# Transposing the attention probabilities on VectorE in 32 by 32 blocks, and a context product split into 32 by 32 array tiles

## What is computed

```
def layer0(x, y, mask, Wq, bq, Wk, bk, Wv, bv):       # one head, masked, 77 keys
    scores = (x @ Wq.T + bq) @ (y @ Wk.T + bk).T
    scores = where(mask == 0, -1e9, scores)
    return softmax(scores) @ (y @ Wv.T + bv) + x

def layer1(query, y, W_qkv, b_qkv, W_o, b_o, gamma, beta):   # 16 heads of 32 channels
    Q, K, V = heads(query @ Wq.T + bq), heads(y @ Wk.T + bk), heads(y @ Wv.T + bv)
    context = softmax(Q @ K.T / sqrt(32)) @ V
    z = join(context) @ W_o.T + b_o + query
    return (z - mean(z)) / sqrt(var(z) + 1e-5) * gamma + beta

out = layer1(layer0(x, ctx, mask, ...), ctx, ...)
```

## Time and profile before

| | us |
|---|---|
| time before, median of 3 runs | 393.39 (391.55 to 395.25) |
| the profiled execution's own time | 394.95 |
| its span, first to last instruction | 393.0 |
| PE busy in the span | 377.4 |
| DVE busy | 295.1 |
| ACT busy | 245.9 |
| POOL busy | 222.0 |

### The profile page before, as it was taken

How to read it: one execution, slowest core, us unless ns; L and a number is a source line. 1 busy time by engine, 2 the same in 40 slices (tenths; PEclk the granted TensorE clock), 3 DMA queues, 4 the chain that set the end, 5 groups by cost and what they waited for, 6 DMA issues and landing times.

```text
span 393.0 us, 11993 instructions
## 1 busy us (share of the span) xinstructions
PE 377.4 (96%) x4860; PEld 286.7 (73%) x4860; DVE 295.1 (75%) x711; ACT 245.9 (63%) x749; POOL 222.0 (56%) x245
## 2 busy tenths in 40 slices
PE   8999998899999999999999999999999999799894
PEld 7878956577777787777777777778777777577663
DVE  0446587568867997799977996799778997457886
ACT  2343778765588666866487558856686648556820
POOL 0520655435647764785578664785478647733541
PEclk9999999999999999999999999999999999899999
DMA  8937410530042322522152224222243113322022
GB/s 309 392 125 231 123 39 20 189 107 4 18 157 98 98 71 65 176 94 64 44 177 77 85 72 155 99 98 72 83 147 118 30 57 92 138 97 71 19 107 107
DMA packets 22461, 42.52 MB, mean 108 GB/s; under 512 B 3685, under 2 KB 5221, under 8 KB 22279
## 3 DMA queue, kind: packets, MB, share of 16 engines
q1 hardware_dynamic: 21866, 41.06, 31.8%
q10 hardware_dynamic: 540, 0.69, 0.5%
HBM read 26.49 MB, written 8.39 MB: 89 GB/s over the span
## 4 chain that ended last, share of the span: by engine, by line
PE 82%; ACT 9%; DMA 4%; DVE 3%; issue 1%; SPq 0%; DVEq 0%
PE ps_q L1035 21%; PE ps_out L1124 21%; PE ps_t L1063 11%; PE ps_s L1049 7%; PE ps_pv L1099 6%; PE ps_out L995 5%; ACT prob L563 3%; ACT y L600 2%; PE ps_s L961 2%; DMA pt<-pt 2%; ACT pt L574 1%; PE ps_s L1142 1%; PE ps_s L974 1%; DMA raw<-in_w0k 1%; ACT q L524 1%
## 5 line engine op out<-in xcount | busy, mean ns | idle before, releaser
L418 POOL TENSOR_TENSOR prob<-prob,rc 128x308 f32<-128x308 f32 x128 | 91.9, 725 | 113.5 <-DVE rc L785 112.8
L563 ACT ACTIVATE prob<-ps_s,mx 128x77 f32<-128x77 f32 x512 | 120.5, 334 | 3.5 <-DVE mx L776 3.3
L574 ACT ACTIVATE pt<-ps_t 122x512 f32<-122x512 f32 (+2 forms) x93 | 55.6, 598 | 56.1 <-PE ps_t L1063 53.0
L783 DVE TENSOR_REDUCE sm<-prob 128x4 f32<-128x308 f32 x128 | 59.5, 465 | 25.6 <-ACT prob L563 25.1
L776 DVE TENSOR_REDUCE mx<-ps_s 128x4 f32<-128x308 f32 x128 | 53.7, 465 | 17.8 <-PE ps_s L1049 17.8
L1063 PE MATMUL ps_t<-ident,prob 128*122 128x128 f32 (+1 forms) x372 | 58.3, 279 | 1.7 <-ACT pt L574 1.6
L392 POOL TENSOR_TENSOR x_l<-x_raw,x_h 128x512 fp32r<-128x512 f32 x32 | 44.4, 1390 | 21.0 <-ACT x_h L506 10.8
L1063 PEld LDWEIGHTS ps_t<-ident,prob 128*122 128x122 f32 (+1 forms) x372 | 46.1, 153 | 13.0 <-issue 3.7
L1035 PE MATMUL ps_q<-x_h,wq_h 128*128 128x512 f32 x128 | 53.4, 417 | 0.0
L1035 PE MATMUL ps_q<-x_h,wq_l 128*128 128x512 f32 x128 | 53.0, 414 | 0.0
L1049 PEld LDWEIGHTS ps_s<-k1T,q 32*64 32x64 f32 x2048 | 26.2, 133 | 28.0 <-issue 15.9
(11 more groups left out here) (134 smaller groups left out, 616.9 us busy)
## 6 DMA issues: line engine op xcount, KB each, us to landing
x_raw<-in_xT SPq DMA_DIRECT2D x14, 512.0 KB, 4.4
y<-in_x SPq DMA_DIRECT2D x28, 256.0 KB, 3.0
out<-y SPq DMA_DIRECT2D x28, 256.0 KB, 2.3
pt<-pt SPq DMA_DIRECT2D x31, 90.0 KB, 2.6
pt<-pt SPq DMA_DIRECT2D x31, 64.0 KB, 2.0
mask_sb<-in_mask SPq DMA_DIRECT2D x8, 154.0 KB, 4.7
raw<-in_w0q SPq DMA_DIRECT2D x4, 256.0 KB, 5.3
x_raw<-in_xT SPq DMA_DIRECT2D x1, 1024.0 KB, 7.7
```

Source lines behind the costliest of these rows:

```text
L418: nc.gpsimd.tensor_tensor(ap, ap, wide(rc[:, k % 2, h], KEYS), ALU.mult).then_inc(prob_done, 1)
L563: e = nc.scalar.activation(prob[:, k % 2, t, h], ps_s[:, h, t * KEYS:(t + 1) * KEYS], ACT.Exp, bias=mx[:, k % 2, h, t:t + 1])
L574: nc.scalar.activation(pt[0:n, c], ps_t[0:n, :], ACT.Copy).then_inc(pt_ready, 1)
L783: nc.vector.reduce_sum(sm[:, k % 2, h], prob[:, k % 2, :, h], AX_X).then_inc(sum_done, 1)
```

## The change

- `prob` and `pt` get three blocks of 32 columns for each head (77 padded to 96; POOL zeroes the 19 padding columns once). DVE transposes two heads at a time for all four tiles in one instruction (`nc.vector.transpose`, 4 x 6 blocks of 32 by 32, 768 elements on each partition), two instructions in a unit. The PE transposes, ACT's moves of `ps_t` and SP's two DMAs in each unit go.
- A 32 by 32 block stays in its quadrant of partitions: after it, each quadrant of 32 partitions holds the keys of its own 32 rows of x. So `v1` is spread to all four quadrants (seven DMAs, once), and the context of a unit is made of 48 products of 32x32 weights and 128 columns: two halves of 24, each with 3 key parts x 2 quadrants x 4 heads. The two quadrants of a half go to two banks (`ps_ab`). Output and query products stand between the halves.
- The sums of the exponentials come from the exponential itself (`accum_out` on ACT); DVE's reduction goes.
- The rounding of x to `x_h` moves from DVE to ACT (4 instructions in a block).
- The context's rounding and rest are queued one step sooner (`round_ct(i, k - 1)`, `ct_rest(i, k - 1)` at the end of step `k`), and the output of block `b - 1` starts in group 0 with 8 of its 56 products. The residual of the fourth tile moves to the head of DVE's step for group 0.
- In unit 0 the projection of V stands ahead of the next unit's query and ACT moves it after the exponentials. The last unit's order is rewritten along the same lines; tiles 2 and 3 of the block before the last go through ACT and POOL like all others.

```diff
-OUT_END = {0: (0, 2, 5, 8), 1: (8, 14, 19, 24), 2: (24, 28, 35, 42), 3: (42, 46, 51, 56)}
-OUT_AT = {1: (0, 14, 18, 22), 2: (22, 28, 36, 42), 3: (42, 44, 51, 56)}
+OUT_AT = {0: (0, 0, 4, 8), 1: (8, 14, 18, 22, 26), 2: (26, 28, 34, 38, 42), 3: (42, 44, 49, 51, 53, 56)}
...
-        pt = sb("pt", [P, CHUNKS, BLOCK])
-        pt_1 = sb("pt_1", [KEYS, BLOCK])
-        prob = sb("prob", [P, 2, TILES, GROUP_HEADS, KEYS])
+        pt = sb("pt", [P, GROUP_HEADS, PARTS, TILES, Q])
+        prob = sb("prob", [P, 2, TILES, GROUP_HEADS, PADDED])
...
                 for t in range(TILES):
-                    e = nc.scalar.activation(prob[:, k % 2, t, h], ps_s[:, h, t * KEYS:(t + 1) * KEYS], ACT.Exp, bias=mx[:, k % 2, h, t:t + 1])
+                    e = nc.scalar.activation(prob[:, k % 2, t, h, 0:KEYS], ps_s[:, h, t * KEYS:(t + 1) * KEYS], ACT.Exp,
+                                             bias=mx[:, k % 2, h, t:t + 1], accum_out=sm[:, k % 2, h, t:t + 1])
...
+            def transposes(i, k, a):            # on VectorE
...
+                own = slice(2 * a, 2 * a + 2)
+                wait(dve, prob_done, heads(i, k, 2 * a + 1) + 1)
+                wait(dve, pv_done, units(i, k))
+                nc.vector.transpose(pt[:, own].rearrange("p h n t r -> p t (h n) r"),
+                                    prob[:, k % 2, :, own].rearrange("p t h (n r) -> p t (h n) r", r=Q)).then_inc(t_done, 1)
...
+            def context(i, k, half):            # on TensorE
...
+                if half == 0:
+                    wait(pe, t_done, pairs(i, k, PAIRS))
+                    wait(pe, ctl_ready, units(i, k))
...
+                for n in range(PARTS):
+                    depth = Q if n + 1 < PARTS else LEFT
+                    for side in range(2):
+                        r = 2 * half + side
+                        keys = slice(r * Q, r * Q + depth)
+                        to = context_of(ps_ab[:, :, 0:CT])[:, side].rearrange("p (t j) r -> p j t r", j=HALVES)[:, half]
+                        for h in range(GROUP_HEADS):
+                            own = slice(g * P + h * HEAD_DIM, g * P + (h + 1) * HEAD_DIM)
+                            mm = nc.tensor.matmul(to[h * HEAD_DIM:(h + 1) * HEAD_DIM], v1[keys, b % 2, slot(r, n), own], pt[keys, h, n],
+                                                  start=(n == 0), stop=(n == PARTS - 1))
...
# TensorE's step: before each unit had scores, three transposes, query, output, context(k - 1); now
+                elif g == 0:
+                    query(i, k + 1, 0, 7)
+                    layer0(i, b + 1)
+                    query(i, k + 1, 7, 12)
+                    context(i, k - 1, 0)
+                    query(i, k + 1, 12, QUERY)
+                    part(1)
+                    context(i, k - 1, 1)
+                    part(2)
+                elif g < 3:
+                    part(0)
+                    query(i, k + 1, 0, 12)
+                    part(1)
...
+                    context(i, k - 1, 0)
+                    query(i, k + 1, 12, QUERY)
+                    part(2)
+                    context(i, k - 1, 1)
+                    part(3)
...
# VectorE's step, its new beginning
+                if g == 0:
+                    residual(i, b - 2, 3)
+                    statistics(i, b - 2, 3)
                 if g == 3:
                     residual(i, b - 1, 2)
...
+                for h in range(GROUP_HEADS):
+                    largest(i, k, h)
+                inverse_sums(i, k, 0)
+                if g == 1:
+                    residual(i, b - 1, 0)
+                if g == 2:
+                    residual(i, b - 1, 1)
+                if g == 3:
                     p0_rest(i, b + 1)
+                transposes(i, k - 1, 0)
+                inverse_sums(i, k, 1)
+                transposes(i, k - 1, 1)
...
+                ct_rest(i, k - 1)
```

523 lines of the change are left out of this document (222 added, 301 removed).

## The result

The changed kernel takes 406.96 us (median of 4 runs, 404.98 to 407.20) against 393.44 for the kernel before (4 runs in the same session): a ratio of 1.033, 95% interval 1.028 to 1.039. The forecast was 379 us, faster, with a range of 368 to 408; the measured time lies near its far end and on the other side of no change. The profiled execution has a span of 405.2 us, 12.2 more than the 393.0 of before.

What follows compares the result with a forecast made beforehand. PE was taken to bound the steady blocks, 42.6 us falling to 41.1. Blocks -10.1, transfer -3.5, opening +1.5 and tail -2.2 made -14.3: span 378.7 of 393.0, 379 on the median, range 368 to 408.

Steps and rivals of the forecast that it cites:

- What bounds the kernel: In the steady blocks PE has no slack; its work sums to 42.4 us a block, which is the window.
- Terms 1 and 2: In a block, three PE transposes in each unit go, 5.6 us, and the old contexts go, 4.4 us.
- Term 5: The context in 32x32 tiles on PE costs 0.88 us a half, 7.0 in a block; dear end 13.2.
- Rival C: Eight small tiles on PE do not run side by side: context 1.62 us a half, 409 in all; chance 0.13.
- Rival A: ACT's accumulate costs its whole small row, 0.205 us more for each exponential: 403 in all; chance 0.14.
- Terms 6 and 7: A DVE transpose takes 0.90 us start to start; an ACT exponential with accumulated sum 0.31 instead of 0.21.
- moving the sums off DVE: DVE's sums, 7.4 us of DVE in a block, are hidden behind PE, so removing them is worth nothing by itself.
- The waits: PE's contexts wait for DVE's second transpose in a block's first unit, partly in the second: 1.5 us a block.
- Term 4: SP's two transfers in each unit go; near the end one cost a 2.02 us wait and lower clock: 3.5 gone.
- Opening: Units 1 to 3 become 8.7 us by ACT, and unit 0 waits 1 to 2 for V's rounding: together +1.5.
- Tail: From the last scores' end to the last tile's statistics: 24.0 us before, 21.7 after, so -2.2.

Runs made afterwards that it cites:

- b: Changed kernel with 8 instead of 24 products in each context half, the other two key parts left out: 383.27 us, ratio 0.971.
- c: Changed kernel with one head of each pair transposed on DVE, the other left out: 405.02 us, ratio 1.029.
- h: Kernel before with `accum_out` on ACT's exponentials and without DVE's sums: 402.48 us, ratio 1.019.
- a: Changed kernel with the sums of the probabilities back on DVE and no accumulated output on the exponentials: 422.34 us, ratio 1.068.
- q: Kernel before with 128 more instructions in PE's stream and the 1 MB load of the last residual rows two units later: 388.99 us, ratio 0.986.
- g: d plus `wo_ready` waited for at 2 before the first output products and both context halves of unit 28 behind its output products: 401.64 us, ratio 1.016.
- d: Changed kernel with SP storing the last-but-one block's fourth tile behind the last block's four stores: 404.54 us, ratio 1.026.
- l: g with another order in the last step of all engines, SP's stores included: 403.43 us, ratio 1.022.
- j: Changed kernel with 128 more instructions ahead of everything in PE's stream: 403.85 us, ratio 1.0225.
- e: Changed kernel with the two context halves back to back, at the second one's place, in every unit: 411.84 us, ratio 1.041.
- i: e with 128 more instructions ahead of everything in PE's stream: 400.42 us, ratio 1.014.
- k: e with 64 more instructions ahead of everything in PE's stream: 410.38 us, ratio 1.041.

## Why the prediction was wrong, point by point

*What bounds the kernel.* Right: PE's work, before and after (b, c). But the sum that stood for it, 42.4 as the window is, gave the handovers to the wrong owners. Start to start over one clean block, added up by form from the timelines:

```
us in one block        full x112  context  scores  layer 0  transposes  together
before                   27.5       4.2      3.5     2.2       4.8        42.2
changed                  29.3       6.9      3.6     2.3       0.4        42.5
```

112 full products are 26.1 at 0.233. The rest, 1.4 before and 3.2 after, is what they lose beside small tiles and transposes, with the short waits.

*Terms 1 and 2, what goes.* Forecast 5.6 + 4.4 = 10.0, measured 4.4 + 4.2 = 8.6 in the columns of the transposes and the context, and 0.7 in the first column (0.08 behind the second and third transposes of each unit): 9.3. The 0.09 ahead of the old context and the 0.08 behind the first transposes stay when these go, since the scores pay them.

*Term 5, the context.* This is the step that failed first: "so I take the scores' end: 0.88 for a half", entry and exit included, although the prediction had "plus some 0.2 of entry and exit" just ahead of it. A half is 0.86 to 0.87 and 0.2 more on the full products: 1.06, 8.5 a block instead of 7.0. Of that 0.030 is each product, against 0.0275 for the scores, and 0.33 is fixed, twice in a unit. The rule quoted there, that a change of tiling mode drains the engine, speaks of just this, and the rows priced it at 0.2, part of which they also show behind the PE transposes; cutting the context in two and parting it from the scores made three such changes of one. Rival C (409 us) came close to the measured 407 by luck: it had a half at 1.62 and PE at 45.5 in a block, where 1.06 and 42.2 were measured, and nothing at the ends. Its mechanism is not what happened: at 0.030 a product, against the 0.062 that it took from layer 0, the small tiles do run side by side. Rival A's 403 is as little borne out, with exponentials at 0.30.

*Terms 6 and 7, transpose and accumulate.* Right in size (0.96, 0.30). That moving the sums off DVE is worth nothing was wrong in both directions: h and a show that ACT has no room for the sums in the kernel before and DVE none in the changed one.

*The waits.* 1.5 a block was forecast; the first unit of a clean block waits 0.2, and c gained 0.15, because PE was not 3 us shorter. Where it was 3.8 shorter (b), 1.0 came. The unit without layer 0 waits 2.7. So the block's two errors had opposite signs: PE's work 2.6 over the forecast's 39.6, the waits 1.3 under.

*Term 4, the transfer.* 3.5 is right for units 28 to 30 (q), and it went. A wait for DVE in the same unit, 2.7 and 1.6 of clock (g), took its place. The text said that the context waits for DVE in a block's first unit; it did not ask what happens in the one that has no layer 0.

*Opening.* +1.5 on units 1 to 3 and -1.5 on 4 to 7 were forecast, +3.4 came: 1.6, 0.5, 1.2 and 1.0 of waits, where the kernel before has 2.7 in all, and a clock of 0.85 from 60 to 80, against a block gain that does not exist. How much of it is the clock stays open.

*Tail.* -2.2 forecast, +5.0 measured, 2.8 of it SP's order (d); of the rest, two of DVE's four last rows at 1.65 instead of 0.75 are 1.8 (read from the rows; l, which tried to mend it, did not). This is the second step that failed: the forecast counted PE's queue and ended at the statistics; POOL's and SP's queues behind it were not followed, although the change moved two tiles' last rows from DVE to POOL.

*Not in the sum at all.* PE's stalls without a releaser, by the evidence above for instructions: 3.1 us in the changed kernel's scores and layer 0 against 0.8 before; 0.8 and 0.3 lie in its fourth block and 1.2 in its fifth, which are 1.0 and 1.1 longer (j has none of them).

## What to carry to other kernels

When PE bounds, count not only products but how often a group of small tiles is entered and left, here 0.2 us each time, and ask of a group that is removed whether its neighbour will go on paying them. Follow every queue to the last store, and look for the one unit in which the work that covers a wait is missing. Before a difference of 1% is put down to a design, move the instruction stream by half a packet and measure again; here that alone was worth 0.8% to the kernel before, and 2.6% to one variant (e, i).

## What the runs showed of the hardware that was not expected

- PE can stand still 0.8 to 2.9 us inside or right behind runs of small instructions, waiting for nothing in the profile, and a shift of the stream by 64 or 128 instructions removes or moves it (e, i, k). The granted clock then is at its lower level for some microseconds behind some of these stalls (0.61 over 168 to 175 in e) and not behind others (1.00 over 259 to 262 in e).
- Two groups of small tiles with a wait on their own engine between them lose 0.15 there, nearly the 0.2 of going in and out (e).
- An accumulated sum on ScalarE shows as a second row of 0.2 to 0.3 us but adds 0.09 to the distance between exponentials.
